# Tables of means and inverse deviations computed inside the stages' rounds, and the last gelu chunk of the last MLP rounded by VectorE

## The reference, cut to what matters

```python
h = tok(x)                                  # patches @ W.T + b, class token, positions
h = h + attn0(layernorm(h))                 # 64 queries on 133 keys, projection
h = h + mlp0(layernorm(h))                  # 192 -> 768, tanh gelu, 768 -> 192
h = h + attn1(layernorm(h))                 # 12 heads of 64, qkv 192 -> 2304
h = h + mlp1(layernorm(h))                  # quantised 192 -> 768 -> 192:
# mlp1: xq = round(clip(x / a1, -8, 7)); x1 = gelu((xq @ wq1.T) * s1 + b1), clipped to +-10
#       hq = round(clip(x1 / a2, -8, 7)); x2 = (hq @ wq2.T) * s2 + b2
```

## Time and profile before

| what | value |
|---|---|
| time before, median of 3 runs | 2626.57 us (2626.11 to 2627.27) |
| the profiled execution: its own time | 2628.79 us |
| its span, first to last instruction | 2627.0 us |
| mean granted TensorE clock | 0.993 of full speed |
| busy: PE 2499.1 us, DVE 2188.3 us, ACT 2098.1 us | 95%, 83%, 80% of the span |
| stages, us from the span's start | to 389; to 785.6; to 2387.7; to 2627 |

### The profile page before, as it was taken

The page is one execution under the profiler, slowest core; times in us unless marked ns, Lnnn a source line. Parts: engine busy times, 40 slices in busy tenths (PEclk is TensorE's granted clock), DMA queues, the critical chain, the costliest instruction groups (busy, mean ns, idle before and its releaser), DMA issues. The chain is left out here.

```text
span 2627.0 us, 83621 instructions
## 1 busy us (share of the span) xinstructions
PE 2499.1 (95%) x27865; PEld 2135.4 (81%) x27865; DVE 2188.3 (83%) x5770; ACT 2098.1 (80%) x6210; POOL 1079.7 (41%) x1501
## 2 busy tenths in 40 slices
PE   5899999999998999999999999999999999998786
PEld 5788867888787888888888888888888888886565
DVE  5766668888867888888888888888888888887997
ACT  4777767777756888888888888888888888886998
POOL 5677733333322333333333333333333333342233
PEclk9999999999999999999999999999999999999999
DMA  6334410000003333333333333333333333330111
GB/s 179 105 110 119 117 28 9 0 0 36 9 1 71 74 80 69 73 79 71 73 77 72 73 76 73 73 75 75 73 73 76 73 72 78 73 71 11 46 41 51
DMA packets 181843, 173.27 MB, mean 66 GB/s; under 512 B 19206, under 2 KB 180432, under 8 KB 181520
## 3 DMA queue, kind: packets, MB, share of 16 engines
q1 hardware_dynamic: 181776, 172.44, 27.7%
HBM read 46.49 MB, written 9.68 MB: 21 GB/s over the span
## 5 line engine op out<-in xcount | busy, mean ns | idle before, releaser
L1404 POOL TENSOR_TENSOR b_pr<-b_pr,b_rinv 128x394 f32<-128x394 f32 (+1 forms) x768 | 626.1, 842 | 990.6 <-DVE b_rinv L1362 990.6
L1299 ACT ACTIVATE b_pr<-b_banks,b_nmx 128x197 f32<-128x197 f32 (+1 forms) x1536 | 627.8, 424 | 37.4 <-DVE b_nmx L1356 28.9
L1356 DVE TENSOR_REDUCE b_nmx<-b_banks 128x2 f32<-128x394 f32 (+1 forms) x768 | 395.8, 557 | 63.2 <-PE b_banks L1224 59.4
L1208 PE MATMUL b_banks<-b_xt,wqkv 128*128 128x197 f16 x3840 | 383.1, 249 | 3.7 <-DVE b_qk L1346 2.4
L1208 PEld LDWEIGHTS b_banks<-b_xt,wqkv 128*128 128x128 f16 x3840 | 317.0, 98 | 35.2 <-issue 18.9
L1234 PE MATMUL b_bank_t<-ident,b_pr 128*128 128x128 f32 (+3 forms) x3072 | 333.8, 250 | 2.8 <-DVE b_pt L1327 2.7
L1224 PE MATMUL b_banks<-b_kst,b_qst 128*128 128x197 f16 (+1 forms) x3072 | 327.3, 249 | 1.6 <-ACT b_pr L1299 1.6
L1299 ACT ACTIVATION_READ_ACCUMULATOR b_pr<-b_banks,b_nmx 128x1 f32 (+1 forms) x1536 | 314.2, 205 | 0.0
L1234 PEld LDWEIGHTS b_bank_t<-ident,b_pr 128*128 128x128 f32 (+3 forms) x3072 | 287.7, 141 | 22.5 <-issue 8.4
L1224 PEld LDWEIGHTS b_banks<-b_kst,b_qst 128*128 128x128 f16 (+1 forms) x3072 | 265.4, 105 | 20.9 <-issue 11.0
L1346 DVE SCALAR_TENSOR_TENSOR b_qk<-b_banks,b_qk 128x394 f16<-128x394 f32 x384 | 216.3, 563 | 56.7 <-ACT b_qk L1284 56.7
(11 more groups left out here) (244 smaller groups left out, 4904.7 us busy)
## 6 DMA issues: line engine op xcount, KB each, us to landing
b_qst<-b_qk SPq DMA_DIRECT2D x512, 147.8 KB, 2.6
b_kst<-b_qk SPq DMA_DIRECT2D x512, 73.9 KB, 2.3
patches<-in_x SPq DMA_DIRECT2D x64, 588.0 KB, 4.3
out<-z_res SPq DMA_DIRECT2D x32, 192.0 KB
out<-z_res SPq DMA_DIRECT2D x32, 103.5 KB
m_raw_weights<-in_wqkv SPq DMA_DIRECT2D x2, 1152.0 KB, 6.9
m_raw_weights<-in_w SPq DMA_DIRECT2D x2, 576.0 KB, 5.3
h<-in_fc SPq DMA_DIRECT2D x1, 768.0 KB, 5.9
```

The costliest lines, as they stand in the source:

```text
L1208: last = t.matmul(out[:, g * SEQ:(g + 1) * SEQ], w[:, (2 * n + g) * P:(2 * n + g + 1) * P], x, start=(j == 0), stop=(j == 4))
L1299: last = nc.scalar.activation(pr[n % 3][0:ROWS[c], c, e, :], banks[0:ROWS[c], c, e * SEQ:(e + 1) * SEQ], ACT.Exp, bias=nmx[n % 2][0:ROWS[c ...
L1356: v.reduce_max(nmx[n % 2][0:ROWS[c], c, :], banks[0:ROWS[c], c, 0:2 * SEQ].rearrange("p (e t) -> p e t", e=2), AX.X, negate=True).then_inc ...
L1404: last = nc.gpsimd.tensor_tensor(p, p, inv, ALU.mult)
```

## The change

`norm_tables` is gone. `norm_part` makes the same tables without ScalarE: instead of a square root and a reciprocal it takes a first guess of the inverse root from the bits of the number and improves it three times. Its instructions come in three to four parts (`variance`, 7 instructions; `key_rows`, 6; `guess`, 5; `refine`, 6) and for the columns of the first 48 images (96 columns) and the last 16 (32 columns) apart. The first 48 images' tables for the next stage are made in the last rounds of the stage before, the other 16 images' in an early round of the stage that uses them:

- for `mlp_0`: the first 48 images in `embed_attend` after the last job (`a1`) of rounds 32 to 35; the others in `mlp_0` as units 19 to 21;
- for `attention_1`: in `mlp_0` as units 29 to 31; the others behind the normalising of images 2 and 3;
- for `mlp_1`: in `attention_1` behind the statistics of images 61 and 62; the others behind `quantise` of pairs 2 and 3.

`rounds` keeps its loop when units stand near the end of a stage. `mlp_1` begins with the scaling of 96 columns and two tiny instructions that make the clip limits of the rounded chunk. TensorE's useless products at the three starts go from 50, 36 and 42 to 24, 6 and 12. In `mlp_1` the last of the six chunks is no longer clipped by VectorE and rounded by ScalarE: VectorE alone does `round_last`, two dependent instructions.

```diff
-    start = max([first - min(shifts)] + [k + 1 for k in tails])
-    turns = (count - max(shifts) - start) // 2
+    late = [k for k in tails if k >= count // 2]
+    start = max([first - min(shifts)] + [k + 1 for k in tails if k < count // 2])
+    turns = (min([count - max(shifts)] + late) - start) // 2
...
+                units.update({count: first_variance, count + 1: lambda: key_rows(dve), count + 2: lambda: guess(dve), count + 3: lambda: refine(dve)})
                 rounds(dve, DVE_ORDER, count, job, {"a1": units}, first=2)
...
+    def improve(dve):
+        then(dve, v.tensor_tensor(tmp[2], rstd, rstd, ALU.mult))
+        then(dve, v.tensor_tensor(tmp[2], tmp[2], tmp[1], ALU.mult))
+        then(dve, v.scalar_tensor_tensor(out=rstd, in0=tmp[2], scalar=1.5, in1=rstd, op0=ALU.add, op1=ALU.mult))
+
+    def guess(dve):
+        then(dve, v.tensor_scalar(tmp[1], tmp[0], -0.5, None, ALU.mult))
+        then(dve, v.tensor_scalar(rstd.bitcast(I32), tmp[0].bitcast(I32), -0.5, ROOT_GUESS, ALU.mult, ALU.add))
+        improve(dve)
+
+    def refine(dve):
+        improve(dve)
+        improve(dve)
...
-                norm_v(dve)
...
+                units.update({19: lambda: variance(dve), 20: lambda: key_rows(dve), 21: roots,
+                              count - 3: lambda: next_variance(dve), count - 2: lambda: next_guess(dve), count - 1: lambda: next_refine(dve)})
...
-                norm_s(act)
...
-                            work(50, 0)
+                            work(24, 0)
...
-                first_steps = {("x", 0): 36, ("q", 0): 7, ("s", 0): 8}
+                first_steps = {("x", 0): 6, ("q", 0): 7, ("s", 0): 8}
...
+                        if isinstance(img, int) and img == 2:
+                            variance(dve)
+                        if isinstance(img, int) and img == 3:
+                            guess(dve)
+                            refine(dve)
...
+                        if isinstance(img, int) and img == n_img - 3:
+                            next_variance(dve)
+                        if isinstance(img, int) and img == n_img - 2:
+                            next_guess(dve)
+                            next_refine(dve)
...
-                norm_v(dve)
-
-                v.tensor_scalar(rstd[:], rstd[:], S["inv_a1"][:, 0:1], None, ALU.mult).then_inc(scaled_rstd, 1)
-                dve.wait_ge(scaled_rstd, 1)
...
+                scale_rstd(slice(0, split), 1)
...
+                    if isinstance(u, int) and 2 * u + b == 2:
+                        variance(dve)
+                    if isinstance(u, int) and 2 * u + b == 3:
+                        guess(dve)
+                        refine(dve)
+                        scale_rstd(slice(split, 2 * n_img), 2)
...
+                def round_last(u, b):
+                    a = act_out[(2 * b + LAST) % 4][:]
+                    dve.wait_ge(gelu_made, chunks_before(u, b) + HC)
+                    v.tensor_scalar(a, a, S["inv_a2"][:, 0:1], ROUND + float(LOW_BITS), ALU.mult, ALU.add).then_inc(last_scaled, 1)
+                    dve.wait_ge(last_scaled, 2 * u + b + 1)
+                    dve.wait_ge(made_y[b], u)
+                    v.tensor_scalar(hid[b][:, LAST, :], a, limits[:, 1:2], limits[:, 0:1], ALU.min, ALU.max).then_inc(last_done, 1)
...
-                                      (clip_hidden(3, 4, 5), 1), (quantise, 3)])
+                                      (clip_hidden(3, 4), 1), (round_last, 1), (quantise, 3)])
...
                 def round_chunk(u, b, f):
-                    n = chunks_before(u, b) + f
-                    act.wait_ge(clipped, n + 1)
+                    if f == LAST:
+                        return
+                    act.wait_ge(clipped, by_scalar(u, b) + f + 1)
...
-                            act.wait_ge(hid_done, n - 3)
+                            if f == 3:
+                                act.wait_ge(last_done, 2 * u + b)
+                            else:
+                                act.wait_ge(hid_done, by_scalar(u, b) + f - (3 if f > 3 else 2))
...
-                        work(42)
+                        work(12)
...
-                    pe.wait_ge(hid_done, chunks_before(u, b) + HC)
+                    pe.wait_ge(hid_done, by_scalar(u, b) + LAST)
+                    pe.wait_ge(last_done, 2 * u + b + 1)
```

More of the change, by code:

```diff
@@ new lines, in _, with first_variance @@
+                room = patches[0][:].rearrange("p k t -> p (k t)")
+                width = 2 * (3 * n_img // 4)
+                variance, key_rows, guess, refine = norm_part(nc, S, n_img, False, [room[:, k * width:(k + 1) * width] for k in range(3)], keys=True)
+                def first_variance():
+                    for m in range(2):
+                        dve.wait_ge(patch_hi[m], count)
+                        dve.wait_ge(patch_split[m], count)
+                    variance(dve)
+                units.update({count: first_variance, count + 1: lambda: key_rows(dve), count + 2: lambda: guess(dve), count + 3: lambda: refine(dve)})
@@ new lines, in _, with norm_part, then, variance @@
+                rounds(dve, DVE_ORDER, count, job, {"a1": units}, first=2)
+def norm_part(nc, S, n_img, later_images, tmp, keys=False):
+    split = 2 * (3 * n_img // 4)
+    cols = slice(split, 2 * n_img) if later_images else slice(0, split)
+    images = slice(split // 2, n_img) if later_images else slice(0, split // 2)
+    v, step, steps = nc.vector, S["norm_step"], S["norm_steps"]
+    st, mean, rstd = S["stats"][:, cols], S["mean"][:, cols], S["rstd"][:, cols]
+    half = D / 2
+    def then(dve, ins):
+        steps[0] += 1
+        ins.then_inc(step, 1)
+        dve.wait_ge(step, steps[0])
+    def variance(dve):
+        then(dve, v.tensor_tensor(mean, st[:, :, 1], st[:, :, 4], ALU.add))
+        then(dve, v.tensor_scalar(mean, mean, 0.5, None, ALU.mult))
+        then(dve, v.tensor_tensor(tmp[0], st[:, :, 1], st[:, :, 4], ALU.subtract))
+        then(dve, v.scalar_tensor_tensor(out=tmp[0], in0=tmp[0], scalar=half / 2, in1=tmp[0], op0=ALU.mult, op1=ALU.mult))
+        then(dve, v.tensor_tensor(tmp[1], st[:, :, 2], st[:, :, 5], ALU.add))
+        then(dve, v.tensor_tensor(tmp[0], tmp[0], tmp[1], ALU.add))
+        then(dve, v.tensor_scalar(tmp[0], tmp[0], 1.0 / D, EPS, ALU.mult, ALU.add))
+    def key_rows(dve):
+        growth, moments = S["growth"][:, cols], S["moments"][:, cols]
+        by_chunk = lambda a: a.rearrange("p (i c) -> p i c", c=2)
+        then(dve, v.tensor_tensor(tmp[1], growth, growth, ALU.mult))
+        then(dve, v.tensor_tensor(tmp[1], tmp[1], moments[:, :, 1], ALU.mult))
+        for rows, c in ((slice(NK1, P), 0), (slice(0, P), 1)):
+            then(dve, v.tensor_scalar(by_chunk(tmp[0])[rows, :, c], by_chunk(tmp[1])[rows, :, c], EPS, None, ALU.add))
+            then(dve, v.tensor_copy(by_chunk(mean)[rows, :, c], moments.rearrange("p (i c) k -> p i c k", c=2)[rows, :, c, 0]))
+    def improve(dve):
[9 more added lines that the diff above has]
+        improve(dve)
+    return variance, key_rows, guess, refine
```

75 lines of the change are left out of this document (28 added, 47 removed).

## The result

| what | before | changed kernel |
|---|---|---|
| median | 2627.07 us (6 runs, 2626.11 to 2628.25) | 2636.57 us (6 runs, 2633.18 to 2638.14) |
| ratio of the times | 1 | 1.0036, 95% interval 1.0026 to 1.0046 |
| profiled execution, its span | 2628.79, 2627.0 us | 2633.18, 2631.4 us |
| busy PE, DVE, ACT | 2499.1, 2188.3, 2098.1 us | 2485.3, 2215.9, 2076.6 us |

The changed kernel is 9.5 us slower (6.8 to 12.1): 0.36%, more than the 0.2% up to which the prediction speaks of no change. The prediction was 2628.4 us and "no change". The result lies in its range of 2614 to 2642, but above the forecast's own 2623 to 2634, and the call of "no change" was missed: a slower kernel had been given 0.35.

A forecast was written before the change was run, and what follows sets the result against it. TensorE bounds `mlp_0` and `attention_1`; in `mlp_1` ScalarE and VectorE are near full. −14.5 + 1.7 + 0 + 7.2 + 5.9 + 3.0 − 1.5 = +1.8 us on the 2626.57 us median gives 2628.4 us, range 2614 to 2642.

The forecast's parts named there:

- Rival 2: TensorE's clock falls more often in `mlp_1`, slower; sign: windows at 0.8 to 0.9 all through; chance 0.15.
- Rival 3: In `mlp_1` VectorE and ScalarE wait for each other: 0.3 us more per round, +8, 2637 us; chance 0.12.
- What is taken away: Table building before the last three stages: 4.5, 5.1 and 4.9 us go, sum −14.5 us.
- `embed_attend`: Table steps behind rounds 32 to 35 partly overrun VectorE's waits: cost 1.7 us, bounds 0 and 2.5.
- `mlp_0`: Inserted units fit VectorE's 2.15 us wait per round for TensorE: cost 0, up to 1 without that cover.
- `attention_1`: Steps behind images 2, 3, 61 and 62 delay TensorE's transposes: cost 7.2 us, bounds 3 and 9.5.
- `mlp_1`, steady rounds: VectorE replaces ScalarE as bound, a round gets 0.21 us longer: +5.9 us over 28 rounds, bounds +4 and +11.
- VectorE's floor of 6.99 us: VectorE's time per `mlp_1` round: floor 6.53 us plus 0.46 for `round_last`, against 6.77 us per round before.
- `mlp_1`, start: First four rounds take up 5.3 us of added work, about half covered by VectorE's idle time: cost 3.0 us.
- `mlp_1`, end: In the last two rounds ScalarE stays the bound and saves 0.51 each; last chunk reaches `down` earlier: −1.5 us.
- Rival 1: ScalarE was `mlp_1`'s bound and its relief shows: −7 us instead of +5.9, 2615.5 us; chance 0.25.
- Rival 4: TensorE takes up the delays in `attention_1`, better covered than read: −4 us, 2624 us; chance 0.12.

The follow-up runs named there:

- e1: Kernel before with only the last MLP's last chunk clipped and rounded by VectorE, tables as before: 2635.35 us against 2626.03, ratio 1.0033.
- e2: Changed kernel with the last chunk rounded by ScalarE as before, so only the tables are moved: 2631.82 us against 2626.03, ratio 1.0019.
- e11: The kernel of e2 run again unaltered, for a second profile and set of times: 2631.51 us against 2627.29, ratio 1.0019.
- e12: Kernel before with only VectorE's order in `mlp_1` changed (`finish` earlier, `quantise` dealt out): 2619.66 us, ratio 0.9973 to before.
- e4: e2 with the table steps in `attention_1` dealt out to VectorE's waits: 2619.26 us against 2626.03 before, ratio 0.9972.

## Why the prediction was right or wrong

The number fell into the range with some luck. The part of the range above 2634 us stood there for rivals 2 and 3, and neither came in that size; what came was two terms of the forecast's own sum that were too small and one with the wrong value. In the unit of the table, changed kernel against before:

| part | predicted | measured |
|---|---|---|
| end of `embed_attend`, start of `mlp_0` | −4.5 + 1.7 | −2.5 |
| `mlp_0` with the start of `attention_1` | −5.1 + 0 | −4.7 |
| `attention_1` with the start of `mlp_1` | −4.9 + 7.2 | +4.9 (six profiles against four) |
| `mlp_1` | +5.9 + 3.0 − 1.5 | +10.7 (244.9 and 244.4 against 233.9) |
| sum | +1.8 | +8.4; by the times +9.5 |

Of the 6.6 us between the two sums 3.3 lie in `mlp_1`, 2.6 in `attention_1` with the start of `mlp_1` and 0.7 in front of that.

**What is taken away** was right to a quarter of a microsecond. The starts lie where the prediction put them, 2.2, 0.1 and 0.7 us behind the first work of the block.

**`embed_attend`: right, and nearly misread.** By the first pair of profiles the steps cost nothing: the block ended at 388.9 us in both. The changed kernel's execution had come 2.0 us earlier to the maximum of that stretch, by chance. From there the stretch is 2.0 us longer (without the 4.5 of the table), predicted 1.7. In the timeline of the changed kernel the rows that answer to the earlier trace rows have no wait left but one:

```profile
363.93 0.30 DVE L648 TENSOR_REDUCE mx<-bank_s 128x1 f32<-128x133 f32 x1 [2.38 <-PE bank_s L489]
...
370.39 0.29 DVE L648 TENSOR_REDUCE mx<-bank_s 128x1 f32<-128x133 f32 x1
...
383.42 0.85 DVE L668 SCALAR_TENSOR_TENSOR o<-bank_o,rinv,o 64x192 f16<-64x192 f32 x2
```

**`mlp_0`: right.** The inserts cost nothing; 4.7 instead of 5.1 us is the removed table.

**`attention_1`: mechanism right, size too small.** Behind image 62 TensorE waited with pair 3's transposes as said, 2.87 us (the row above; predicted 3.0). Behind images 2, 3 and 61 the changed kernel has these waits of TensorE, none of which the kernel before has:

```profile
816.89 1.03 PE L1231 MATMUL b_banks<-b_xt,wqkv 128*128 128x197 f16 x10 [1.47 <-DVE b_qk L1371]
...
843.14 1.03 PE L1231 MATMUL b_banks<-b_xt,wqkv 128*128 128x197 f16 x10 [1.36 <-DVE b_qk L1371]
...
845.47 0.89 PE L1257 MATMUL b_bank_t<-ident,b_pr 128*128 128x128 f32 x8 [0.49 <-DVE b_pt L1347]
...
2344.84 0.88 PE L1257 MATMUL b_bank_t<-ident,b_pr 128*128 128x128 f32 x8 [1.57 <-DVE fc L1347]
```

That is 1.5, 1.9 and 1.6 us against the predicted 0.4, 2.0 and 1.8. The term that was too small is the one behind image 2, where the pipeline was to be "not full yet": its 1.6 us of steps were late almost whole. In the round of image 3 most of the wait fell on an earlier job (`b_qk`), not on the transposes. In all, without falls of the clock, the bursts cost 8.5 us, predicted 7.2 with a bound of 9.5. The mean of 10.4 includes 2 us of falls, for which the sum had no term in this stage.

**`mlp_1`, steady rounds: the number right, the reason for the kernel before not.** VectorE's floor of 6.99 us met the 6.97 of the trace. This is the round that answers to the earlier trace rows, VectorE, then the addition on GpSimd that stretches the two clips:

```profile
2473.10 0.87 DVE L1534 TENSOR_SCALAR z_act<-z_act,q_hi,q_lo 128x394 f32<-128x394 f32 x2
2473.89 1.01 DVE L1549 TENSOR_TENSOR z_res<-z_bank_y,q_scale 128x384 f32<-128x384 f32 x2
...
2475.69 1.79 DVE L1534 TENSOR_SCALAR z_act<-z_act,q_hi,q_lo 128x394 f32<-128x394 f32 x2
2477.41 0.41 DVE L1539 TENSOR_SCALAR z_act<-z_act,inv_a 128x394 f32<-128x394 f32 x1
2477.86 0.48 DVE L1542 TENSOR_SCALAR z_hid<-z_act,z_limits 128x394 f32<-128x394 f32 x1
...
2480.07 0.87 DVE L1534 TENSOR_SCALAR z_act<-z_act,q_hi,q_lo 128x394 f32<-128x394 f32 x2
```

```profile
2475.09 2.17 POOL L1562 TENSOR_TENSOR z_res<-h,z_res 128x384 f32<-128x384 f32 x2 [4.80 <-DVE z_res L1549]
```

Both new instructions come behind the addition, as the prediction's order had it. But the 6.77 us of the kernel before were left as a number between two floors (6.53 and 6.48) that explained neither. They were the cycle of 13.54 us over two pairs. The prediction looked for the busiest engine and walked one round; the cycle is two rounds long and runs through three engines, none of them full.

**`mlp_1`, start: the term was too small.** e1 has the last chunk without the steps and e2 the steps without the last chunk: 239.5 − 233.9 = 5.6 us for the one (predicted 5.3: 5.9 + 0.9 − 1.5; e1's one fall more and its shorter start nearly cancel), and 4.5 to 5.4 for the other (e2 and e11 against before, changed kernel against e1; predicted 2.1). The prediction counted half of the inserted time as covered by the idle 5.0 us of a window. That idle time stood in pieces of at most 1.0 us between the gelus, most of them 0.6, and the steps in two lumps of 1.6 and 2.7 us behind `quantise`, where ScalarE then waited, as its two rows show:

```profile
2400.23 0.62 ACT L1589 ACTIVATE z_hid<-z_act,inv_a 128x394 f32<-128x394 f32 x1 [2.12 <-DVE z_act L1534]
...
2409.56 0.63 ACT L1589 ACTIVATE z_hid<-z_act,inv_a 128x394 f32<-128x394 f32 x1 [3.25 <-DVE z_act L1534]
```

**`mlp_1`, end: wrong.** Predicted −1.5, measured 0: from the last `quantise`'s rounding to the end both take 23.83 us. In the last pair three clips beside GpSimd's addition take 2.64 us, and `round_last` stands behind them; that this alone eats up the relief of ScalarE is not shown.

**The rivals.** Rival 1 (ScalarE's relief shows) did not come, and could not: even with GpSimd's addition gone the pair stayed at 6.75 us, since the relief of 0.52 meets the 0.46 that `round_last` adds on the same way. Rival 2 (the clock) came in small: two falls between 2420 and 2600 us instead of one, 2.6 us against 1.5, and its sign, windows at 0.8 to 0.9 all through `mlp_1`, did not show (0.98 over the 180 us). What brings a fall about in these rounds is shown by no run. Rival 3 did not come: VectorE waited 2.2 us in 180 for gelus, while ScalarE's waits (0.83 us per pair, 23.9 us in 180) were for `up`, and not for clips, as the forecast had it. Rival 4 was on the wrong side.

Open: why e1 and e2 add up to more than the change (+0.33% and +0.19% against +0.36%). The intervals (0.2 to 0.46, 0.1 to 0.28, 0.26 to 0.46) allow for it, and no run settles it. How much a fall costs is known in the steady rounds of `mlp_1`, 1.3 to 1.5 us; in `attention_1` only roughly, 0.4 to 2.4.

## What to carry to other kernels

Where two engines are nearly full and neither is, follow one resource with a single buffer from release to release, over as many rounds as it takes to come back to the same engine: that length divided by the rounds is the bound, and reordering the same instructions (8 us in e12) is worth more than moving one from one engine to the other. Idle time in a window is a sum of pieces: work that is put in fits only piece by piece, so deal out dependent steps one by one to the waits that the timeline shows (8.4 us in `attention_1` between e2 and e4). And before a stage of one profile is compared with that of another, look at a stretch in which the code is the same: here it moved by 6 us.

## What the runs showed of the hardware that was not expected

- The same code up to the maximum of `embed_attend` took 354.3 to 360.1 us in fourteen executions. The mean granted clock between 60 and 150 us was 0.94 in the five shortest (up to 354.8) and 0.89 in the two longest (from 359.9), 0.91 or 0.92 between; which of the two brings the other is not shown.
- A pair of 128x394 float32 clips on VectorE took 0.87 us alone and 1.79 beside an addition of 2.17 us on GpSimd; with the addition gone from GpSimd it was 0.87 again, and the time of the kernel fell by 4 us only (2636.57 to 2632.48), because the cycle of 13.51 us for two pairs stood right behind VectorE's own 13.94. The Trainium skill, GPSIMD Engine Reference, Specifications, says that GpSimd shares its SBUF interfaces with VectorE and contends with VectorE's instructions in a two-port mode. The trace agrees, if these clips run in such a mode, which no trace here shows.
- One fall of TensorE's clock in a steady round of `mlp_1` made one pair 1.3 us longer in the changed kernel (8.27 instead of 6.97) and 1.5 in the kernel before (8.18 instead of 6.65). Useless products that kept the clock at 1.00 through 180 us of `mlp_1` gave back 2 us by one pair of profiles and nothing that the times show.
